# Expert weights at a register's address, and a copy on VectorE in place of a transfer per block

## The reference

```python
B, T, D, H, E = (16, 2048, 128, 256, 8)
...
logits = xf @ gate_w + gate_b
probs = jax.nn.softmax(logits, axis=-1)
top2_vals, top2_idx = jax.lax.top_k(probs, 2)
cw = jnp.zeros((N, Ee), dtype=xf.dtype).at[jnp.arange(N)[:, None], top2_idx].add(top2_vals)

def step(acc, params):
    w1, bb1, w2, bb2, we = params
    h = jax.nn.gelu(xf @ w1 + bb1, approximate=False)
    y = h @ w2 + bb2
    return (acc + we[:, None] * y, None)
```

## Time and profile before

| what | us |
|---|---|
| median of 3 runs | 468.99 |
| lowest and highest run | 468.41, 469.1 |
| span of the profiled execution | 509.4 |
| the block stage in it, from the first scatter of results to the last landing | 350 to 484 |

### The profile page before, as it was taken

How to read it: one execution, slowest core, us unless ns; L and a number is a source line. 1 busy time by engine, 2 the same in 40 slices (tenths; PEclk the granted TensorE clock), 3 DMA queues, 4 the chain that set the end, 5 groups by cost and what they waited for, 6 DMA issues and landing times.

```text
span 509.4 us, 10322 instructions
## 1 busy us (share of the span) xinstructions
PE 354.1 (70%) x2395; PEld 291.2 (57%) x2395; DVE 223.3 (44%) x988; ACT 194.9 (38%) x526; POOL 227.9 (45%) x351
## 2 busy tenths in 40 slices
PE   1996459897889788878689797218767667768300
PEld 1354358776768677677577586117656456557200
DVE  5915037765566666575646564601111211202156
ACT  2344126454453535435344534023323323323144
POOL 3003013664646555565536463503664565555600
PEclk9996669998898999999979988657888989879755
DMA  8173712232222232222422221266545455454088
GB/s 211 38 208 104 223 56 58 83 116 71 66 69 66 70 115 59 69 67 69 117 59 66 69 72 40 67 111 187 167 139 183 148 164 194 146 183 163 9 243 251
DMA packets 77471, 58.50 MB, mean 115 GB/s; under 512 B 9276, under 2 KB 68481, under 8 KB 77445
## 3 DMA queue, kind: packets, MB, share of 16 engines
q1 hardware_dynamic: 70213, 49.03, 33.6%
q0 software_dynamic: 4544, 8.44, 5.0%
q10 hardware_dynamic: 2688, 0.75, 0.9%
HBM read 30.70 MB, written 15.58 MB: 91 GB/s over the span
## 4 chain that ended last, share of the span: by engine, by line
SPq 36%; PE 24%; issue 17%; DMA 8%; another core or an unknown queue 5%; ACT 3%; DVE 3%; POOL 2%; ACTq 0%; DVEq 0%; POOLq 0%
SPq L423 26%; PE bank L1303 6%; PE bank L1292 6%; PE bank L1410 4%; PE bank L1419 2%; SPq L413 2%; DMA x<-in_x_tiles 2%; DMA wide<-result 2%; POOL result L640 2%; SPq L463 1%; PE bank L1256 1%; DMA routed<-padding_sb 1%; DMA fold_sb<-in_fold 1%; SPq L478 1%
## 5 line engine op out<-in xcount | busy, mean ns | idle before, releaser
L1292 PE MATMUL bank<-S,xwin 100*128 100x144 f32 x512 | 87.7, 311 | 35.4 <-ACT samp L735 22.9
L640 POOL DMA_INDIRECT result<-y,to x78 | 76.8, 984 | 77.1 <-DVE to L1168 52.2
L1303 PE MATMUL bank<-filt_sb,samp 128*128 128x128 f32 x576 | 86.7, 301 | 14.1 <-ACT samp L735 13.5
L1292 PEld LDWEIGHTS bank<-S,xwin 100*128 100x128 f32 x512 | 71.7, 200 | 40.4 <-ACT samp L735 27.3
L1303 PEld LDWEIGHTS bank<-filt_sb,samp 128*128 128x128 f32 x576 | 77.3, 210 | 27.4 <-ACT samp L735 23.2
L735 ACT ACTIVATE samp<-bank 128x432 f32<-128x432 f32 (+1 forms) x96 | 46.8, 490 | 103.2 <-PE bank L1292 93.5
L584 POOL DMA_INDIRECT routed<-payload,slot x64 | 63.1, 986 | 24.6 <-issue 13.9
L1410 PE MATMUL bank<-rowsT,w_blk 128*128 128x256 f32 x156 | 50.9, 456 | 31.6 <-ACT rowsT L799 20.6
L1176 DVE TENSOR_TENSOR y<-bank,w_blk 128x256 f32<-128x256 f32 x39 | 16.5, 424 | 119.1 <-PE bank L1419 78.1
L561 POOL TENSOR_TENSOR rest<-hat 128x180 f32<-128x180 f32 x32 | 17.0, 531 | 108.5 <-ACT hat L692 108.5
L900 DVE TENSOR_TENSOR S<-ysp,bank 100x512 f32<-100x512 f32 (+1 forms) x96 | 52.5, 550 | 28.4 <-ACT ysp L706 22.4
(11 more groups left out here) (110 smaller groups left out, 499.6 us busy)
## 6 DMA issues: line engine op xcount, KB each, us to landing
xwin<-xpad SPq DMA_DIRECT2D x256, 50.0 KB
w_blk<-w_all SPq DMA_DIRECT2D x39, 321.0 KB
rows_in<-routed SPq DMA_DIRECT2D x39, 129.0 KB
wide<-result SPq DMA_DIRECT2D x16, 256.0 KB, 4.8
w_all<-in_experts SPq DMA_DIRECT2D x4, 642.0 KB
xpad<-wide SPq DMA_DIRECT2D x16, 128.0 KB, 2.9
out_tiles<-res SPq DMA_DIRECT2D x8, 256.0 KB, 4.2
wide<-in_x_rows SPq DMA_DIRECT2D x3, 512.0 KB, 9.0
```

What stands on the lines that cost most here:

```text
L640: nc.gpsimd.indirect_dma_start(result, bass.IndirectOffsetOnAxis(to[:, slot, j:j + 1].bitcast(U32), 0), y[:, slot, j, :], None, bounds_che ...
L1292: last = nc.tensor.matmul(bank[5 + (par + g) % 2][:, i * TAPS * TT:(i + 1) * TAPS * TT], xwin[:, par, t, :], weights[:, t], start=True, st ...
L1303: last = nc.tensor.matmul(bank[7][:, 0:C], samp[:, par, j, :], filt_sb[:, order[j], :], start=(j == 0), stop=(j == TAPS - 1))
```

## The change

The layout of `w_all` changes: up weights, up bias, down bias, down weights, so that the first 386 floats are what is copied and the last 256 what isn't. `w_blk` holds the 386 alone.

- SP no longer transfers weights. It reads the row numbers of two blocks at a time and issues their row transfers, and it begins with the register load only after the waits for the padding rows and the scatters. Its loop body covers 4 blocks in place of 8.
- DVE gets a second result of the plan, `blk_w`, the expert's number for each block. For each block it reads that number into a register, waits until the addition that last used the slot is done, and copies the 386 floats from `w_all` to the slot, two blocks ahead (`AHEAD = 2`). The copy for block i + 2 stands before the addition of block i.
- PE reads the expert's number into a register for each block, before the down product, and takes the down weights straight from `w_all` at the register's address. The up product waits for DVE's copy in place of the transfer.
- POOL and ACT do what they did.

```diff
-W_UP = HID + HALVES
-WROW = W_UP + HALVES * C + C
+W_B2 = HID + HALVES
+W_DOWN = W_B2 + C
+WROW = W_DOWN + HALVES * C
+AHEAD = 2
...
-        w_blk = sb("w_blk", [P, RING, WROW])
+        w_blk = sb("w_blk", [P, RING, W_DOWN])
...
+        def expert_of(eng, turn, place):
+            _, (e,) = nc.values_load_multi_w_load_instructions(
+                blk_w[0:1, bass.ds(turn * RING + place, 1)], engines=[eng], min_val=0, max_val=EXPERTS - 1)
+            return e
...
-            def load_weights(turn, place, row):
-                i, slot, uses = block_at(turn, place)
-                expert = nc.s_assert_within(row >> REGION_BITS, 0, EXPERTS - 1)
-                at_least(sp, s.y_done, i - (RING - 1))
-                sp.dma_start(w_blk[:, slot, :], w_all[:, expert, :]).then_inc(w_arrived[slot], 16)
...
+            def load_group(turn, n):
+                for place in range(0, n, 2):
+                    for at, row in enumerate(first_rows(turn, place, min(2, n - place))):
+                        load_rows(turn, place + at, row)
+
+            sp.wait_ge(s.plan_ready, 2)
             sp.wait_ge(s.idle_written, 16)
             sp.wait_ge(s.scat_even, 32 * (BANDS // 2))
             sp.wait_ge(s.scat_odd, 32 * (BANDS // 2))
             sp.wait_ge(s.pads_written, 16 * EXPERTS)
-            load_rows(0, 0, row)
-            load_rows(0, 1, *first_rows(0, 1, 1))
-            load_blocks(0, range(1, RING))
...
+            block_loop(sp, load_group)
...
+            nc.vector.tensor_scalar(blk_w[:, :], blk_e[:, :], float(EXPERTS - 1), None, ALU.min).then_inc(s.plan_ready, 1)
...
+            def copy_weights(turn, place):
+                i, slot, _ = block_at(turn, place)
+                e = expert_of(mybir.EngineType.DVE, turn, place)
+                at_least(dve, s.y_done, i - (RING - 1))
+                nc.vector.tensor_copy(w_blk[:, slot, :], w_all[:, e, 0:W_DOWN]).then_inc(s.w_ready, 1)
+
+            def block_group(turn, n):
+                for place in range(n):
+                    if not isinstance(turn, int) or turn * RING + place + AHEAD < BLOCKS:
+                        copy_weights(turn, place + AHEAD)
+                    finish(turn, place)
+                    if not is_last(turn, place):
+                        keep_dest(turn, place + 1)
...
             def up(turn, place):
                 i, slot, uses = block_at(turn, place)
-                pe.wait_ge(w_arrived[slot], uses * 16 + 16)
+                pe.wait_ge(s.w_ready, i + 1)
...
             def down(turn, place):
                 i, slot, uses = block_at(turn, place)
+                e = expert_of(mybir.EngineType.PE, turn, place)
                 pe.wait_ge(s.h_ready, i * HALVES + HALVES)
...
                         last = nc.tensor.matmul(bank[slot][:, BLOCK + j * C:BLOCK + (j + 1) * C],
                                                 hid[:, slot, h, j * P:(j + 1) * P],
-                                                w_blk[:, slot, W_UP + h * C:W_UP + (h + 1) * C],
+                                                w_all[:, e, W_DOWN + h * C:W_DOWN + (h + 1) * C],
                                                 start=(h == 0), stop=(h == HALVES - 1))
```

More of the change, by code:

```diff
@@ L322, in program, with block_loop @@
         REST = BLOCKS - TURNS * RING
-        def block_loop(eng, step):
-            for place in range(RING):
-                step(0, place)
+        def block_loop(eng, group):
+            group(0, RING)
             with eng.Fori(1, TURNS) as turn:
[L328 to L331, removed]
+                group(turn, RING)
+            group(TURNS, REST)
+        def expert_of(eng, turn, place):
+            _, (e,) = nc.values_load_multi_w_load_instructions(
+                blk_w[0:1, bass.ds(turn * RING + place, 1)], engines=[eng], min_val=0, max_val=EXPERTS - 1)
+            return e
         def previous(turn, place):
@@ L479, in load_rows @@
                              ).then_inc(rows_arrived[slot], 16)
[L481 to L493, removed]
-            load_weights(0, 0, row)
+            def load_group(turn, n):
[3 more added lines that the diff above has]
+            sp.wait_ge(s.plan_ready, 2)
             sp.wait_ge(s.idle_written, 16)
@@ L1174, in finish, with block_group @@
                 at_least(dve, sent[slot], uses * (16 * SUBS))
-                b2_row = w_blk[:, slot, WROW - C:].unsqueeze(1).broadcast_to([P, SUBS, C])
+                b2_row = w_blk[:, slot, W_B2:W_DOWN].unsqueeze(1).broadcast_to([P, SUBS, C])
                 nc.vector.tensor_tensor(y[:, slot, :, :], bank[slot][:, BLOCK:2 * BLOCK].rearrange(
                     "p (j c) -> p j c", c=C), b2_row, ALU.add).then_inc(s.y_done, 1)
-            def block_step(turn, place):
-                finish(turn, place)
-                if not is_last(turn, place):
-                    keep_dest(turn, place + 1)
+            def copy_weights(turn, place):
[3 more added lines that the diff above has]
+                nc.vector.tensor_copy(w_blk[:, slot, :], w_all[:, e, 0:W_DOWN]).then_inc(s.w_ready, 1)
+            def block_group(turn, n):
+                for place in range(n):
+                    if not isinstance(turn, int) or turn * RING + place + AHEAD < BLOCKS:
+                        copy_weights(turn, place + AHEAD)
+                    finish(turn, place)
+                    if not is_last(turn, place):
+                        keep_dest(turn, place + 1)
+            dve.wait_ge(s.plan_ready, 2)
+            dve.wait_ge(s.experts_loaded, 16 * (EXPERTS // 2))
+            for first in range(AHEAD):
+                copy_weights(0, first)
             keep_dest(0, 0)
-            block_loop(dve, block_step)
+            block_loop(dve, block_group)
             dve.wait_ge(s.share_step, 3)
@@ L1420, in down, with block_group @@
                                                 hid[:, slot, h, j * P:(j + 1) * P],
-                                                w_blk[:, slot, W_UP + h * C:W_UP + (h + 1) * C],
+                                                w_all[:, e, W_DOWN + h * C:W_DOWN + (h + 1) * C],
                                                 start=(h == 0), stop=(h == HALVES - 1))
                 last.then_inc(s.y_psum2, 1)
-            def block_step(turn, place):
-                up(turn, place)
-                if not is_last(turn, place):
-                    transpose_rows(turn, place + 1)
-                if not is_first(turn, place):
-                    down(*previous(turn, place))
+            def block_group(turn, n):
+                for place in range(n):
+                    up(turn, place)
+                    if not is_last(turn, place):
+                        transpose_rows(turn, place + 1)
+                    if not is_first(turn, place):
+                        down(*previous(turn, place))
             transpose_rows(0, 0)
-            block_loop(pe, block_step)
+            pe.wait_ge(s.plan_ready, 2)
+            pe.wait_ge(s.experts_loaded, 16 * (EXPERTS // 2))
+            block_loop(pe, block_group)
             down(TURNS, REST - 1)
```

21 lines of the change are left out of this document (7 added, 14 removed).

## The result

The changed kernel takes 472.1 us in the median of 20 runs (470.26 to 475.75), the kernel before 470.05 us beside it (467.49 to 474.56). The ratio is 1.005, with a 95% interval of 1.0029 to 1.0071: 2.05 to 2.35 us slower, depending on whether medians or ratio are taken, and 1.4 to 3.3 us by the interval. The profiled execution of the changed kernel spans 471.5 us and took 473.35 us from outside.

What follows compares the result with a forecast made beforehand. The prediction took POOL's scatters, 2.57 us a block, to bound the block stage. Its terms, 0 + 1.2 + 0 + 1.8 + 0 + 0 = +3.0 us on 468.99, gave 472.0 us, with a range of 458.5 to 483.

Steps and rivals of the forecast that it cites:

- What bounds the kernel: Block stage: POOL's two scatters per block, 1.284 us each, 2.57 us a block, 100.2 us for 39 blocks.
- the 33 us of stalls: POOL's waits for a block in the first profile's block stage; thought likelier absent from unprofiled runs.
- The 39 weight transfers: Expert weight transfers removed from the block stage: hidden behind POOL, gain 0, bounds 0 and 8.7 us.
- weights are waited for in the runs too: Rival, block stage: PE's 8.7 us of weight waits go, giving 461.5 us; chance 0.22.
- the weight traffic causes the stalls: Rival, block stage: up to 33 us go, down to 437 us; chance 0.09.
- SyncE's start: Block stage's start: SP's register load now follows the padding wait, delaying the first scatter; +1.2 us, bounds 0.5 to 2.
- DVE's load: DVE's added register load, wait and copy per block: 1.7 us a block, below POOL's 2.57; cost 0.
- The copy and POOL at SBUF: DVE's copies hold up POOL's scatters at the SBUF port: +1.8 us, bounds 0 and 15.6.
- PE's register load: PE's load per block and register-addressed down matmuls: load hidden, 0.26 us exposed, block about 2.25 us, cost 0.
- PE becomes the bound: Rival, block stage: PE's register load is not covered, a block passes 2.57 us, giving 482.0 us; chance 0.12.
- The sum: Whole kernel: the terms add to +3.0 us on the median of 468.99, giving 472.0 us.
- the port term: The +1.8 us taken for DVE's copies and POOL's scatters meeting at SBUF.

Runs made afterwards that it cites:

- e1: The kernel before, unchanged, profiled a second time: ratio 1.0008 of before, profiled span 468.9 us.
- e3: The kernel before without the weight transfers of blocks 4 to 38 and the waits for them: ratio 1.0008.
- e5: The kernel before with only the first of each block's two scatters issued and two plain transfers filling the result beforehand: 465.06 us, 0.9918.
- e6: The changed kernel with only the first of each block's two scatters issued and two plain transfers filling the result beforehand: 456.47 us, 0.9712.
- e8: The kernel before with 38 idle matmuls ahead of the first transposes and block 0's down product ahead of block 1's up product: ratio 1.003.
- e10: The kernel before with 52 idle matmuls ahead of the first transposes and block 0's down product ahead of block 1's up product: ratio 0.999.
- e2: The changed kernel with the first two row numbers read ahead of the wait for the padding rows: ratio 1.001 of before.
- e11: The changed kernel with the first row numbers read ahead of the padding wait and 52 idle matmuls on PE: 466.97 us, 0.9946 of before.
- e12: The changed kernel with early row numbers and 52 idle matmuls, the same kernel as e11 measured once more: 467.23 us, 0.996 of before.
- e4: The changed kernel with two more DVE copies of 386 floats per block into an unread scratch tile: ratio 1.0045 of before.
- e7: The kernel before with 38 idle matmuls on PE ahead of the first transposes: ratio 0.9998.
- e9: The kernel before with 52 idle matmuls on PE ahead of the first transposes: ratio 0.9984.

## Why the prediction was right

The forecast of 472.0 us was met, with its sign. By its steps:

*What bounds the kernel.* Right: POOL's 1.284 us per scatter sets the stage, 100.2 us by the prediction's sum and 100.19 in e1 (the prediction counts 78 pitches, the stream 77 and one scatter; the pitch is 1.288 us, so the two come out alike). The reading that the 33 us of stalls don't exist in the runs was right (e1), and so was the sum of what is missing: 32.98 us in the stream, and the first scatter starts 350.56 - 342.94 = 7.6 us earlier, where 7 had been left. The forecast for the profiled span, 504 to 512, was wrong for the same reason: it took the stalls as something that every profile would show. The changed kernel's is 471.5.

*The 39 weight transfers.* Taken as 0 with bounds 0 and 8.7 us; 0 in e3. The upper bound was no fantasy: e5 against e6 gives 8.6 us where POOL is out of the way, and e8 and e10 show waits for weights that reach POOL once it starts 2 us earlier. The rival "weights are waited for in the runs too" had the waits right (10.3 us in e1) and their place wrong: under POOL. With the stalls gone, "the weight traffic causes the stalls" has nothing left to explain.

*SyncE's start.* Taken as +1.2, with the right mechanism; the traces show 1.02 to 1.04 (the distance from the end of SP's wait to the issue, and e2). That the first scatter came 1.20 us later than in e1, and the rows' issue 1.42, meets the forecast partly by chance, as the padding rows landed 0.40 us later after `count` in that execution. The second row transfer does land later, but the chain doesn't wait for it. The median of a load in the changed kernel is what the prediction read off L463:

```profile
L467 SPq TENSOR_LOAD <-blk_i x20: 277/472/637, 332.0 to 425.6; - x20
```

*DVE's load.* Cost 0 was right. The copy takes 0.364 us in the median for the 0.4 estimated, and the register load 0.310 for the 0.48 taken over from SP (ns min/median/max). With the register operations behind the load the step is not cheaper than forecast, though: DVE idles 24.9 us ahead of 36 copies in the stage, 0.69 us each, where 0.68 had been taken.

```profile
L1170 DVE COPY w_blk<-w_all x39: 360/364/637, 329.0 to 432.4; 128x386 f32 x39
...
L334 DVEq TENSOR_LOAD <-blk_w x39: 301/310/415, 327.9 to 431.6; - x39
```

PE does wait for the copy, 9.7 us in 15 waits, the longest 1.1, though it was to come 5.1 us ahead; the stream has no gap there, so it costs nothing while POOL is the bound.

*The copy and POOL at SBUF.* The term that was mis-sized: +1.8 taken, 0.34 measured as the whole growth of the stream (0.26 to 0.52 with e2, e11 and e12). What failed is the step that says who waits. The prediction read off that a scatter wants the port from about 0.5 us on, and let a copy that reaches over that point hold up POOL. The changed kernel's trace shows that it is the copy that waits there. Two scatters, on POOL, and the copies that begin 0.41 us into the first and 0.53 us into the second, on DVE:

```profile
352.82 0.98 POOL L624 DMA_INDIRECT result<-y,to  x1 [0.30 <-DVE to L1154]
...
413.69 0.98 POOL L624 DMA_INDIRECT result<-y,to  x1 [0.30 <-DVE to L1154]
```
```profile
353.23 0.36 DVE L1170 COPY w_blk<-w_all 128x386 f32 x1 [0.70 <-issue]
...
414.22 0.64 DVE L1170 COPY w_blk<-w_all 128x386 f32 x1 [0.63 <-issue]
```

Seven of the 39 copies begin 0.53 to 0.74 us into a scatter. They take 0.43 to 0.64 us in place of 0.36, all end 0.19 us after the scatter, and the scatter keeps its 0.98. Twelve begin 0.04 to 0.42 us into one, and neither they nor the scatter take longer. So the reading of the earlier trace rows was right as far as it went, and its price for POOL was wrong.

What does cost POOL is a copy that is already running when a scatter starts. Four reach more than 0.13 us into one: 0.15, 0.16, 0.22 and 0.29 us. Their scatters take 1.00, 1.02, 1.08 and 1.15 us, together 0.30 us more than four of 0.984, nearly the whole 0.34 us. The longest, on POOL and on DVE:

```profile
381.22 1.15 POOL L624 DMA_INDIRECT result<-y,to  x1 [0.30 <-issue]
```
```profile
381.15 0.37 DVE L1170 COPY w_blk<-w_all 128x386 f32 x1 [0.93 <-issue]
```

In all four the scatter ends 0.85 us after the copy. e4 has 30 such scatters; each ends 0.85 to 0.87 us after the copy that ran across its start, and together they are 1.76 us longer than 30 of 0.984, which is the whole growth of e4's stream against e1. The prediction's sum has no such case.

The Trainium skill's "SBUF — State Buffer", section "Who interferes with whom", has the second comer blocked for the whole of the first one's instruction. Where the copy is first, the trace is near to that: the scatter waits for the copy's end, less the 0.13 us that it can do without it. Where the scatter is first, it isn't so: by the rule the copy at 353.23 would have waited for 0.57 us, and it ran at once. The rule is too strong for such scatters: its effect is in the trace, at 0.34 us in 39 blocks (e4: 1.42 us more with 78 more copies), not at 14 or 28.

*PE's register load.* Hidden, as forecast; no gap of POOL comes of it. The load took 0.30 us in the median, not 0.48, and the down product at a register's address is no slower than at a fixed one, 1.06 us. The block in a burst is 347.49 - 345.51 = 1.98 us, as before the change, and 2.09 us in e6, where PE is the bound; 2.25 had been forecast, and the 0.26 us taken as exposed don't show in the burst. "PE becomes the bound" (2.57 us per block) was far off. In the changed kernel:

```profile
345.51 1.03 PE L1410 MATMUL bank<-rowsT,w_blk 128*128 128x256 f32 x4
...
346.60 1.06 PE L1420 MATMUL bank<-w_all,hid 128*128 x8
...
347.49 1.06 PE L1410 MATMUL bank<-rowsT,w_blk 128*128 128x256 f32 x4
```
```profile
L334 PEldq TENSOR_LOAD <-blk_w x39: 297/301/436, 339.8 to 433.9; - x39
```

*The sum.* The traces give 1.02 + 0.34 = 1.36 us, where +3.0 was forecast and 2.05 to 2.35 measured, with 1.4 to 3.3 as the interval. The 1.36 us stand at the interval's lower edge, and the remaining 0.7 to 1.0 us stay unexplained. One place for them is open: `count` starts at 317.16 to 320.78 us in the changed kernel, e2, e4, e11 and e12, and at 315.30 to 318.72 in e1, e3 and e7 to e10. The change has no part in the work ahead of `count` that would say why, and these single executions overlap, so no run decides it. The sign and the mechanism of SyncE's start were forecast; that 472.0 meets 472.1 so closely is luck: the runs of before beside it have a median of 470.05, 1.06 us above the three that the forecast started from, and the port term was 1.5 us too large.

## What to carry to other kernels

Find the engine whose steady pitch sets the stage before you price a transfer: the weights' waits were 10.3 us in the trace and worth nothing while POOL, at 1.288 us a scatter, was the bound; once it was not, the same change was worth 8.6 us. Where a profile disagrees with the runs by more than a few us, take a second one before you explain its gaps. Measure a start from the event that releases it, since a distance from an earlier mark can hide another wait of a microsecond. And look at the start of a stage that a steady engine bounds: what comes earlier there counts, but only if the next blocks follow at that engine's pitch (e8 and e10 against e11).

## What was not expected of the hardware

*PE's clock at the start of the stage* went with how long PE had been idle after the matmuls put ahead. The first up product (4 matmuls of 128x256) took 2.05 us after 4.45 us of idleness (e7), 1.96 after 3.76 (e8), 1.50 after 2.25 (e9), and 1.10 after 1.66 (e10), 1.43 (e11) and 0.79 (e12). The granted share was 0.50 in e7, fell from 1.00 to 0.50 inside the product in e8 and e9, and was 1.00 in e10 and e11, that is 1.2 and 2.4 GHz. In e9 it fell while PE was at work, 1.6 us after the idle time was over, and before PE's wait of 0.90 us for weights. At 1.00 in e11, it stayed there through the chain's waits of 0.56 us. These are single executions; that idle time alone decides isn't shown.

*A copy at a register's address* on DVE and matmuls at such an address on PE run as fast as at fixed ones: 0.364 us against 0.364 and 0.355 for the two copies at fixed addresses in e4, and 1.06 us for 8 matmuls in both kernels. What it costs is the engine's time ahead of it: a load of 0.31 us on DVE and 0.30 on PE (SP: 0.47), with register operations behind it, 0.69 us of idleness per copy on DVE.

*Copies beside scatters* cost POOL 0.009 us each in the changed kernel and 0.018 for each added one in e4. A copy that starts 0.53 to 0.74 us into a scatter is itself held until 0.19 us after it; one that starts earlier in it runs free; one that runs across a scatter's start holds the scatter up by what it reaches beyond the first 0.13 us.
